# Where the destination term of the first graph attention is added, who splits the second weight, and one planned order for start and loop

## The reference

```
h   = relu(layernorm(x))
# GAT layer 1: 4 heads of 128
xl  = h @ W1;  asrc = <xl, a_src>;  adst = <xl, a_dst>
e   = leaky_relu(asrc[source] + adst[destination], 0.2)
att = softmax over sources of where(mask, e, -1e9)
h1  = elu(att^T @ xl + b1)
# GAT layer 2: 1 head of 256, the same form with W2; its result is added to x
x1  = x + gat2(h1)
# attention: 8 heads of 32
h2  = relu(layernorm(x1))
y   = relu(softmax(where(adj, q k^T / sqrt(32), -inf)) v) @ Wo
out = x1 + y
```

## Time and profile before

| what | before |
|---|---|
| median of 3 runs | 763.39 us (761.03 to 764.08) |
| profiled execution | 763.64 us, of it 761.9 us span |
| PE busy | 689.3 us, 90% (8657 matmuls) |
| DVE busy | 677.6 us, 89% |
| ACT busy | 621.9 us, 82% |
| POOL busy | 577.8 us, 76% |
| PE clock granted, mean | 0.982 |

### The profile page before, as it was taken

How to read it: one execution, slowest core, us unless ns; L and a number is a source line. 1 busy time by engine, 2 the same in 40 slices (tenths; PEclk the granted TensorE clock), 3 DMA queues, 4 the chain that set the end, 5 groups by cost and what they waited for, 6 DMA issues and landing times. The chain is left out here.

```text
span 761.9 us, 27375 instructions
## 1 busy us (share of the span) xinstructions
PE 689.3 (90%) x8657; PEld 572.9 (75%) x8657; DVE 677.6 (89%) x2037; ACT 621.9 (82%) x1929; POOL 577.8 (76%) x796
## 2 busy tenths in 40 slices
PE   0478999999999999999999999999999999999761
PEld 0256888888888888888888788888888888888541
DVE  5978899999999999999999999999999999988641
ACT  0267998888899889998889989999988989889531
POOL 4666888888888878888888888888888878886431
PEclk9999999999999999999999999999999999999985
DMA  6211557766656675665756657556576666645553
GB/s 210 52 26 39 99 113 113 126 122 121 113 120 118 125 120 116 123 116 126 118 114 127 117 125 114 121 125 123 120 119 120 119 125 121 111 97 85 99 90 63
DMA packets 270428, 84.77 MB, mean 111 GB/s; under 512 B 242896, under 2 KB 269904, under 8 KB 270288
## 3 DMA queue, kind: packets, MB, share of 16 engines
q1 hardware_dynamic: 269856, 82.24, 56.8%
q10 hardware_dynamic: 432, 0.79, 0.4%
HBM read 15.86 MB, written 8.39 MB: 32 GB/s over the span
## 5 line engine op out<-in xcount | busy, mean ns | idle before, releaser
L575 ACT ACTIVATE e<-bank,nmx,q_power 128x128 f32<-128x128 f32 x512 | 185.8, 468 | 13.0 <-DVE nmx L911 9.8
L424 POOL TENSOR_TENSOR e_split<-e,e_split 128x512 f16<-128x512 f32 x128 | 148.5, 1160 | 10.3
L436 POOL TENSOR_TENSOR rstd<-var,minus_half 128x1 f32<-128x1 f32 x128 | 72.1, 564 | 70.3 <-DVE var L774 51.2
L1000 PE MATMUL bank<-w_split,hT 128*128 128x260 f16 x768 | 98.8, 279 | 2.3 <-issue 2.2
L519 ACT ACTIVATE eT<-lr,nmx 128x128 f32<-128x128 f32 x256 | 99.2, 392 | 0.1
L1000 PE MATMUL bank<-w_split,h_split 128*128 128x258 f16 x768 | 95.7, 273 | 3.6 <-POOL h_split L407 1.9
L1000 PE MATMUL bank<-h2T,proj_split 128*128 128x128 f16 x1536 | 97.3, 220 | 1.7 <-DMA h2T<-h_split 1.0
L414 POOL TENSOR_TENSOR eTn<-eT,rs 128x512 f32<-128x512 f32 x64 | 66.6, 1041 | 39.7 <-DVE rs L902 39.7
L1000 PEld LDWEIGHTS bank<-h2T,proj_split 128*128 128x128 f16 x1536 | 90.7, 98 | 4.4 <-DMA h2T<-h_split 1.9
L422 POOL CAST e_split<-e 128x512 f16<-128x512 f32 x128 | 78.2, 611 | 20.5 <-ACT e L575 19.2
L1000 PEld LDWEIGHTS bank<-w_split,h_split 128*128 128x128 f16 x768 | 72.5, 97 | 18.5 <-issue 7.4
(11 more groups left out here) (137 smaller groups left out, 1982.8 us busy)
## 6 DMA issues: line engine op xcount, KB each, us to landing
x_in<-in_x_dram SPq DMA_DIRECT2D x64, 128.0 KB, 2.5
out_dram<-x_out SPq DMA_DIRECT2D x64, 128.0 KB, 1.9
adj_in<-in_adj_dram SPq DMA_DIRECT2D x64, 64.0 KB, 2.0
e3T<-e_split SPq DMA_TRANSPOSE x128, 3.2
hT<-h_split SPq DMA_TRANSPOSE x64, 2.5
h2T<-h_split SPq DMA_TRANSPOSE x64, 2.7
attT<-att_split SPq DMA_TRANSPOSE x64, 3.0
w<-in_L_gnn_W_dram SPq DMA_DIRECT2D x2, 256.0 KB, 6.1
```

The costliest lines, as they stand in the source:

```text
L424: pool.tensor_tensor(e3_split[:, g.two, half, 1], e, e3_split[:, g.two, half, 0], ALU.subtract).then_inc(s[low_set], 1)
L436: pool.tensor_tensor(rstd[:, g.two, which:which + 1], var[:, g.two, which:which + 1], minus_half[:, :], ALU.pow).then_inc(s[rstd_set], 1)
L575: ins = act.activation(e3[:, g.two, h, :], S[:, h // 4, (h % 4) * N:(h % 4 + 1) * N], ACT.Exp, bias=nmx3[:, g.two, h:h + 1], scale=q_power ...
L1000: ins = pe.matmul(out_, left, right, start=n == 0, stop=n == len(pairs) - 1)
```

## The change

It has four parts.

1. The matmul of 512 columns for adst in `scores1` is gone, with the second half of the `pick` constant. DVE, in `ab_low`, writes adst times the weight's power of two to a new tile `a_dst` (128 x 4), and `gat1_leaky` adds it as ScalarE's bias. A bias is one number per partition and the heads have different ones, so the leaky relu is now four instructions of 128 columns, where it was one of 512.
2. The halves of W2 no longer come from DVE: ACT writes the high half and a scaled copy (into `prod2`, no longer used by then), POOL subtracts (`w2_high`, `w2_low`).
3. All five tables have a new order and new phases, start and loop in one table.
4. The PSUM banks are given out anew, and with them the PE functions' extra waits.

The number of products, the precision and the DMAs are otherwise the same.

```diff
-        pick = sb("pick", [128, 2, H, 128], F16)
+        pick = sb("pick", [128, H, 128], F16)
+        w2_scaled = prod2.rearrange("p a c -> p (a c)")[:, 0:H * (D + 2)].rearrange("p (k c) -> p k c", k=H)
+        a_dst = sb("a_dst", [128, 2, H])
...
@@ SP @@
-                (e3_transpose_last, 11), (e3_transpose_first, 11), (att_transpose, 12), (load_x, 1), (norm2_transpose, 9),
+                (e3_transpose_first, 10), (e3_transpose_last, 10), (load_x, 0), (load_adj, 2), (store, 11),
...
@@ GpSimd @@
+            @once
+            def w2_low(g):
+                pool.wait_ge(s["w2_high"], 2)
+                pool.wait_ge(s["w2_scaled"], 2)
+                pool.tensor_tensor(w2_split[:, 1], w2_scaled, w2_split[:, 0], ALU.subtract).then_inc(s["w2_low"], 1)
...
+                (split_low0, 11), (e3_first_halves, 13), (picks, 6), (split_low1, 11), (diagonal2, 10), (e3_last_halves, 13),
...
@@ ScalarE @@
+            @once
+            def w2_high(g):
+                act.wait_ge(scale_set["w2"], 1)
+                for j, part in enumerate((slice(0, D), slice(D, D + 2))):
+                    act.activation(w2_split[:, 0, :, part], w2[:, :, part], ACT.Copy, scale=scale[:, 6 + j:7 + j]).then_inc(s["w2_high"], 1)
+                    act.activation(w2_scaled[:, :, part], w2[:, :, part], ACT.Copy, scale=scale[:, 6 + j:7 + j]).then_inc(s["w2_scaled"], 1)
...
-                act.activation(lr[:, g.two, :], Z[:, :], ACT.Prelu, scale=power[:, 1:2], alpha=SLOPE).then_inc(s["lr_set"], 1)
+                done(act, s["dst_set"], g)
+                for h in range(H):
+                    ins = act.activation(lr[:, g.two, h * N:(h + 1) * N], Z[:, h * N:(h + 1) * N], ACT.Prelu, bias=a_dst[:, g.two, h:h + 1],
+                                         scale=power[:, 1:2], alpha=SLOPE)
+                ins.then_inc(s["lr_set"], 1)
...
@@ VectorE @@
-                for part, split, factor in parts:
-                    dve.tensor_scalar(split[:, 0], part, factor, None, ALU.mult).then_inc(s["w2_high"], 1)
-                dve.wait_ge(s["w2_high"], 2)
-                for part, split, factor in parts:
-                    dve.scalar_tensor_tensor(out=split[:, 1], in0=part, scalar=factor, in1=split[:, 0],
-                                             op0=ALU.mult, op1=ALU.subtract).then_inc(s["w2_low"], 1)
...
             def ab_low(g):
+                free(dve, s["lr_set"], g)
+                dve.tensor_scalar(a_dst[:, g.two, :].rearrange("p (a c) -> p a c", a=2), XL[:, :, HF // 2 + 2:HALF], power[:, 1:2], None,
+                                  ALU.mult).then_inc(s["dst_set"], 1)
...
@@ TensorE @@
-                pe.matmul(Z[:, :], abT[:, g.two, :], pick[:, 1].rearrange("p h m -> p (h m)"), start=False, stop=False)
                 for h in range(H):
-                    ins = pe.matmul(Z[:, h * N:(h + 1) * N], pick[:, 0, h, :], abT[:, g.two, :], start=False, stop=h == H - 1)
+                    ins = pe.matmul(Z[:, h * N:(h + 1) * N], pick[:, h, :], abT[:, g.two, :], start=False, stop=h == H - 1)
...
+                after(pe, s["en_set"], g, 0)
```

More of the change, by code:

```diff
@@ L352, in picks @@
             def picks(g):
-                pool.memset(pick[:, :, :, :], 0.0).then_inc(s["pick_set"], 1)
-                for n in range(4):
-                    side, row = pick[:, n % 2].rearrange("p (a c) m -> p a c m", a=2), 2 * H * (n // 2) + 2 * (n % 2)
+                pool.memset(pick[:, :, :], 0.0).then_inc(s["pick_set"], 1)
+                for n in range(2):
+                    side, row = pick.rearrange("p (a c) m -> p a c m", a=2), 2 * H * n
                     pool.wait_ge(s["pick_set"], n + 1)
@@ L598, in _ @@
             steps(lambda graphs: run([
-                (gat2_copy, 9), (att_copy, 12), (relu1, 4), (gat1_copy, 7), (abT_copy, 6), (qk_copy, 10), (split_high2, 7),
-                (elu_exp, 7), (gat1_leaky, 6), (gat2_leaky, 8), (split_high3, 7), (split_high0, 6), (h1_high, 7), (relu2, 9),
-                (v_copy, 10), (gat1_exp, 6), (gat2_exp, 8), (mha_exp_last, 10), (split_high1, 6), (mha_exp_first, 10),
+                (split_high3, 12), (gat1_copy, 9), (relu1, 6), (qk_copy, 12), (abT_copy, 8), (elu_exp, 9), (gat2_leaky, 10),
+                (gat1_leaky, 8), (gat2_exp, 10), (relu2, 11), (h1_high, 9), (gat1_exp, 8), (v_copy, 12), (gat2_copy, 10),
+                (mha_exp_first, 12), (w2_high, 8), (att_copy, 13), (split_high0, 10), (mha_exp_last, 12), (split_high1, 10),
+                (split_high2, 11),
             ], graphs))
@@ L927, in _ @@
             steps(lambda graphs: run([
[L928 to L933, removed]
+                (mha_max, 12), (w2_shift, 9), (gat1_recip, 8), (ab_high, 7), (v_low, 12), (ab_low, 7), (att_norm, 13),
+                (xl_evac, 7), (att_low, 13), (proj_scale, 9), (norm1_apply, 5), (gat2_recip, 10), (w2_sums, 7), (ab2_evac, 9),
+                (norm1_moments, 4), (proj_largest, 8), (w1_row, 5), (residual1, 10), (xl2_evac, 9), (b1_prep, 6),
+                (norm2_moments, 10), (relu1_low, 5), (variance1, 4), (variance2, 10), (w1_products, 1), (w1_scale, 5),
+                (qk_low, 11), (elu, 8), (w1_largest, 0), (gat2_scores, 9), (norm2_apply, 10), (gat1_scores, 7),
+                (residual2, 13), (w1_sums, 4), (proj_row, 8), (w2_row, 7), (relu2_low, 10), (w2_scale, 7),
             ], graphs))
@@ L1033, in mha_av @@
                 done(pe, s["vv_set"], g)
-                after(pe, s["h1T_set"], g, 4)
+                after(pe, s["lr_set"], g, 5)
                 at_ends(pe, s["attT_set"], g, -1)
-                after_once(pe, power_set["proj"], g, 6)
                 for j in range(NH):
@@ L1089, in qk @@
                 pe.wait_ge(h2T_here[g.two], g.dma2)
-                after(pe, s["x_out_set"], g, -3)
+                after(pe, s["ab_set"], g, 4)
+                after(pe, s["xl_set"], g, 4)
                 at_ends(pe, s["qkT_set"], g, -1)
-                after_once(pe, power_set["w1"], g, 9)
                 for c in range(4):
@@ L1100, in transpose2 @@
                 done(pe, s["eT2_set"], g)
-                after(pe, s["ab_set"], g, 3)
-                after(pe, s["xl_set"], g, 3)
-                at_ends(pe, s["abT_set"], g, 2)
+                after(pe, s["x_out_set"], g, -4)
+                after_once(pe, power_set["w2"], g, 1)
+                at_ends(pe, s["ab2_set"], g, 0)
+                at_ends(pe, s["xl2_set"], g, 0)
                 at_ends(pe, s["en2_set"], g, -1)
@@ L1170, in project_out @@
                 pe.wait_ge(attT_here[g.two], g.dma2)
-                after(pe, s["qkT_set"], g, 2)
+                after(pe, s["ab2_set"], g, 4)
+                after(pe, s["xl2_set"], g, 4)
+                after_once(pe, power_set["w2"], g, 5)
                 at_ends(pe, s["x_out_set"], g, -1)
-                after_once(pe, power_set["w1"], g, 11)
+                at_ends(pe, s["en2_set"], g, 3)
                 split_matmul(WO[:, 0:D], [
@@ L1187, in _ @@
             steps(lambda graphs: run([
-                (qk, 10), (spread_w2, 7), (aggregate2, 9), (transpose_ab, 6), (scores1_mask, 6), (aggregate1, 7),
-                (spread_proj, 6), (scores1, 6), (scores3_mask, 10), (scores2, 8), (w2_ones, 7), (scores3_first, 10),
-                (project_v, 10), (scores3_last, 10), (project1, 5), (mha_av, 11), (spread_w1, 1), (project_out, 12),
-                (turn_w2, 6), (project2, 7), (turn_w1, 0), (turn_proj, 4), (transpose2, 8), (transpose1, 6),
+                (turn_w1, 0), (spread_proj, 2), (spread_w1, 0), (turn_w2, 1), (project1, 0), (mha_av, 6), (spread_w2, 1),
+                (project2, 2), (aggregate2, 3), (transpose1, 1), (qk, 4), (transpose_ab, 0), (aggregate1, 1),
+                (scores1_mask, 0), (scores2, 2), (scores1, 0), (scores3_mask, 4), (scores3_first, 4), (project_out, 6),
+                (scores3_last, 4), (project_v, 4), (turn_proj, 1), (transpose2, 2), (w2_ones, 1),
             ], graphs))
```

107 lines of the change are left out of this document (53 added, 54 removed).

## The result

The changed kernel takes 765.72 us (median of 22 runs, 763.39 to 769.51), the kernel before, run beside it, 763.21 us (22 runs, 760.67 to 765.92): a ratio of 1.0041, 95% interval 1.0029 to 1.0053. That is slower by 0.4%: less than the 0.5% set as no change, though with this many runs the interval leaves out 1. It is 8 us over the forecast of 757.6. The profiled execution took 766.4 us, its span 764.4.

A forecast was written before the change was run, and what follows sets the result against it. PE bounds the kernel before; after, a ring through ACT's leaky relus was to set 10.53 us per step. From 763.64 us, 3.7 less in the loop and 2.1 at the start give 757.8, as median 757.6; range 747 to 767.

The forecast's parts named there:

- The loop: 57 steps of the graph loop: each from 10.595 to 10.53 us, 3.7 us less in all.
- start and filling: Before the 7th h1T: first h1T 4.5 us earlier, filling 2.4 us longer, together 2.1 us less, bounds 0 and 5.
- the end: After the loop: the last graph waits on DMA landings and order as before, 0 us change, within 2.
- the 0.105 us of hold-ups: Loop step: lateness beyond the 10.49 us clean step, taken to vanish because the new SP order issues attT earlier.
- this ring: ACT and DVE: `elu_exp`, leaky relus, `gat1_scores`, `residual2`, `mha_max`, exponentials, `gat1_copy`, PE's `aggregate1`, next `elu_exp`: 10.53 us per step.
- The second ring of the prediction: Exponentials, POOL's halves, DMA transpose, PE from `mha_av` to `aggregate1`: 21.06 us over two graphs, 10.53 us per step.
- e3T: DMA-transposed tile PE waits for at `mha_av`: no hold-ups counted; waits over 0.1 us per graph would show the second rival.
- PE keeps setting the pace: Rival: leaky relus take 0.27 us, the ACT ring falls under PE's 10.27, 743 to 749 us; chance 0.18.
- The saving goes into waits: Rival: hold-ups of 0.1 us stay, step 10.6 to 10.65 us, 763 us (760 to 767); chance 0.26.
- Slower: Rival: ACT becomes the bound, four leaky relus at 0.37 us each, step 10.74, 769.6 us; chance 0.14.
- 0.347 forecast from the exponential: ACT's leaky relus in `gat1_leaky`: 0.347 us each, 1.39 us for four, 0.82 more than before.
- six of its 0.04 and 0.05 us between engines: Assumed signal times between engines in the first ring; the forecast is wrong if they are off by half.

The follow-up runs named there:

- end waits everywhere: Changed kernel with the PE waits that guard the first and last 14 graphs issued for all 64 graphs: 770.83 us, ratio 1.0093 to the kernel before.
- `residual2` first: Changed kernel with `residual2` issued ahead of `gat1_scores` on DVE: 758.69 us, ratio 0.9948 to the kernel before.
- `residual2` moved both ways: Changed kernel with `residual2` ahead of `gat1_scores` on DVE (758.69 us), or moved later, behind `relu2_low` (786.71 us).
- in the old layout: Kernel before with part 1 alone, its tables, banks and weight preparation kept: 795.46 us, ratio 1.042, and 795.73 us in a second run.

## Why the prediction was wrong

**The direction, by terms.** The loop was to give 3.7 us and took 6.1; start and filling were to give 2.1 and took 2.4; the end, put at 0, gave 6.0. The step without hold-ups was forecast at 10.53 and came out at 10.50 to 10.51, the mean at 10.701. So the step of the prediction that failed in the sum is "I take it that this removes the 0.105 us of hold-ups": they grew to 0.19 us, 11 us over 57 steps where I had set 0. One half of its reason came true: the waits for attT in the loop, 5.9 us before, are gone. Others came in their place. A part is shown: the end waits make the commonest step 0.16 us longer in the 21 outer steps of the 57, at most 3.4 us, or 1.9 us at the 0.09 that the run with end waits everywhere gave on average. Before, the outer steps were hardly longer than the inner ones (10.62 against 10.59 us on average); now these waits stand in the ring. The rest, 0.14 to 0.16 us per graph, contains late landings of h2T, before which the weight load idles 5.3 us in ten waits. In the profiles of the changed kernel's variants the rest lies between 0.07 and 0.17 us per graph, so its size isn't settled. With `residual2` first the same wait is 1.8 us in five, which fits `relu2_low`, the last before h2T's transpose, no longer being behind `residual2`. What makes the rest of the hold-ups stays open.

**The ring.** "So this ring takes 10.53 us whatever PE saves" was right in its start, ACT's four leaky relus, and wrong in its path. That 10.53 lies so near the measured 10.50 is luck: it is the length of another ring. On the path over `mha_max`, DVE is ahead by 0.15 us (its nmx3 is listed 0.23 us, not 0.50 as in the earlier trace rows), and ACT's queue is ahead of PE by 0.23 us at `aggregate1`. The second ring of the prediction, through the DMA transposes, doesn't bind either: the waits of the loop name none for e3T. The ring that binds was not looked for: the new wait in `transpose2` stood in the kernel after, and I read it as a buffer rule, not as an edge from DVE to PE. The runs with `residual2` moved both ways show it. No run gives ET2 another bank with the rest kept, so the price of that edge alone is known only by way of `residual2`.

**The rivals.** "PE keeps setting the pace" needed leaky relus of 0.27 us, and they took 0.343. The edge to `transpose2` isn't the whole of it: with `residual2` first, where PE no longer waits there, the step is still 10.44, over PE's own 10.15. "The saving goes into waits" (760 to 767 us) has the measured time, and is right in that hold-ups kept the loop from gaining, but its sign, waits for e3T, isn't there, and the ring is another. "Slower" was to decide once a step is over 10.70; the mean is 10.701, but not by leaky relus of 0.37 us.

**The prices.** Four leaky relus from 404.98 to 406.35 are 0.343 us each (0.347 forecast from the exponential). The Trainium skill's page *ScalarE: Activation LUTs*, section "What ACT_TABLE_LOAD costs", gives an estimate of 0.386 by its rule for two pointer operands; the trace doesn't agree. PE saves its 0.22 us and idles it away (the matmul back: +1.3 us, by the ratios +0.6, within the noise). The prediction says that six of its 0.04 and 0.05 us between engines stand in the first ring; its sum has four.

**The start.** The first `project1` came at 24.30 as said, the first h1T at 43.9 and not at 41.6:

```profile
24.30 2.78 PE L1018 MATMUL bank<-w_split,hT 128*128 128x260 f16 x12 [6.93 <-DVE w_split L689]
```

```profile
36.76 0.16 DVE L644 TENSOR_SCALAR power<-bank 128x2 f32<-128x2 f32 x1 [1.70 <-PE bank L997]
...
37.63 0.18 DVE L917 RECIPROCAL rs<-sm 128x4 f32<-128x4 f32 x1
...
43.89 0.75 DVE L818 SCALAR_TENSOR_TENSOR h1T<-ex,h_scale,bank 128x512 f32<-128x512 f32 x1 [1.61 <-ACT ex L551]
```

Only a part of DVE's freed time became speed: it waits 1.70 us for PE to spread W2's largest values and 1.61 us for `elu_exp`. The first of these waits lies on the path to h1T: `gat1_recip` (L917) stands behind it on DVE and starts at 37.63, though ACT has its sums ready at 36.32. The six steps of filling cost 4.6 us more, not 2.4: with part 1 undone they are 102.9 - 43.4 = 59.5, so the leaky relus make 2.1, and the new tables the other 2.5 (59.5 against 57.0).

**The end.** Its -6.0 us were not forecast. Without part 1 the end is 47.9 us, so it comes from the tables and banks; which entry of them brings it wasn't tried. From the last h1T on, PE waited 14.9 us for e3T at `mha_av` and 3.8 for attT at `project_out` before; after, it idles 5.6 at `mha_av` and 9.1 for attT.

**What the change is.** Its two halves go against each other: the bias, as four instructions in this order, costs 18 us (32 in the old layout), tables, banks and weight preparation gain 16. I had put both into one sum, and so neither was seen.

## What to carry to other kernels

When a change moves tiles to other banks or buffers, write down each wait that is new as an edge (who sets it, who stands behind it) and walk every ring through it; the one with the longest instruction that changed is the first candidate. A bound engine that gets shorter pays only if no ring is within its saving: look for engines that each wait once per graph for the next. And try the parts apart, since an order tuned for one instruction length (four leaky relus) can be wrong for another (one).

## What the runs showed of the hardware

Waits that are already satisfied are not free on PE when they stand behind one that held it up: with six of them between the wait for `x_out` and `project1` (three ahead of `transpose2`'s matmul, three behind it), the time from the end of `residual2` to `project1` grew from 0.28 to 0.44 us, all of it behind `transpose2`. The price of one isn't shown. A Prelu of 128 columns with bias and scale as tiles takes 0.343 us from start to start, so four take 1.37 us where one of 512 columns took 0.57.
